# Folding the row normalisation into the attention phase that follows it

## The chip, the core and the metric

The kernel runs on one core of a Trainium2 chip. The metric is the device time of one launch in microseconds (us), here the median of several runs on one chip. The core has five engines that run their own instruction streams and meet at semaphores: TensorE (PE in the profile, with its weight loads as PEld), VectorE (DVE), ScalarE (ACT), GpSimd (POOL) and SyncE (SP), whose stream here holds only DMA issues.

## The reference

Two layers, each a cross attention added to the residual rows and a feed-forward part added to them, over x of 4 batches, 512 rows, 256 columns, and a context of 4 batches, 1024 rows, 192 columns. Each part reads normalised rows:

```python
def _layernorm(x, axis=-1, eps=1e-05):
    m = jnp.mean(x, axis=axis, keepdims=True)
    v = jnp.var(x, axis=axis, keepdims=True)
    return (x - m) / jnp.sqrt(v + eps)

# each layer, in outline
x = x + attention(_layernorm(x), context)   # 16 heads of 64; q = xn @ w_q, k, v from the context; out @ w_o + b_o
x = x + ffn(_layernorm(x))                  # layer 0: 32 experts, top 6, and 2 shared; layer 1: 8 experts, top 1, and a shared one
```

Attention is softmax(q k^T / 8) v per head. Its output bias b_o is added to every row. All data are float32.

## The kernel before

**Phases.** The program is a row of phases, each a block of its own on all engines: a normalisation (`norm_phase`, tag `n_`), attention of layer 0 (`attention_phase`, tag `L0a_`), a normalisation (`L0n_`), the experts of layer 0 (`L0e_`), a normalisation (`L1i_`), attention of layer 1 (`L1a_`), a normalisation (`L1n_`), and the experts of layer 1. A phase begins when the one before it has ended on every engine. The residual rows stay in SBUF as `xres`, 128 partitions by 16 tiles of 256; four tiles are one batch. The two normalisations ahead of the attentions, `n_` and `L1i_`, are the ones that the change takes away.

**norm_phase.** DVE takes `bn_stats` of all 16 tiles (L201), then combines them in small chained operations to a mean, a variance (L213 to L220), and, after a square root on ACT (L169), to a reciprocal with one Newton step and a shift (L222 to L228). The tiles are normalised in 8 groups of two, the even tile on DVE (L234), the odd one on ACT (L165). PE transposes a group with 4 transposes into one PSUM bank (L192). ACT copies the bank, rounded to float32r, into `xnT_hi` (L176), and DVE writes the rest, bank minus `xnT_hi`, into `xnT_lo` (L243). All products of the kernel are made of such high and low parts in three float32r matmuls. In `n_` SP loads x in two halves and the context of batch 0, which ACT (L158) and POOL (L151) split.

**attention_phase.** 32 segments, for 4 batches times 8 pairs of heads. Segment i does the attention of pair i and prepares pair i+1 and i+2. PE's order in a segment, written out by hand: transpose of the last tile of row maxima (`transpose_max`, L680), queries of i+1 (L598, six matmuls), eight `qk` steps (L696, L697) with the value projections of the next pair of segments between them, the output projection of i-1 into banks 7 and 6, then four `score` steps of i+1 (L674). A score step fills four banks, and a DVE `reduce_max` (`maximum`, L524) must have read them before the next score step may start. Between the scores lie the products with v (`pv`, L711) as `FILL` says, and after score 1 the two key projections of i+2 (ACT copies them in `high_keys` L437, DVE subtracts in `low_keys` L516). `total` (L721) ends the segment. On DVE a segment is `low_keys`, `normalise` (L529, L532), `high_queries` L503, `high_output` L538, `low_queries` L508, `low_output` L542, `add_output` L550 twice, and the four maxima with another `low_keys` ahead of the last. `add_output(i-1)` waits for the output projection.

**Start of the attention.** SP loads the packed weights of segment n into one buffer `raw`, which ACT rounds (`high_weights`, L427) and POOL subtracts (`low_weights`, L378); the load of the next one waits for that. POOL first writes rows of -1 (L413, four memsets). PE then makes keys 0, queries 0 (waiting for `low_weights(1)` and `low_keys(0, 0)`), values 0 and 1, score 0, and so on. After the four maxima of pair 0, ahead of segment 0, DVE adds the output bias to all 16 tiles of `xres` in four operations of 1024 columns (L584), from a buffer that shares its place with `inv`.

Of the kernel before, what the change touches and what calls it, by code (L numbers as in the profile page):

```python
# [7 lines left out]
ALU = mybir.AluOpType  # L8
# [4 lines left out]
P = 128  # L13
# [33 lines left out]
def build(nc, x, ctx_top, ctx_bot, layer_in, out):  # L47
# [6 lines left out]
    with stack:  # L54
# [30 lines left out]
        def norm_phase(tag, xres, source=None, keep=None, wipe=None, clear=(), prefetch=None):  # L85
# [6 lines left out]
            NCH = 2  # L92
            with scope() as s:
# [11 lines left out]
                if source is not None:  # L105
                    stage = sb(s, tag + "stage", [P, NCH, SKV])
                if wipe is not None:
                    zeros = sb(s, tag + "zeros", [P, DIM])
                sem = norm_sems | sems(
                    s, tag, ("x0 x1 id chi clo " + " ".join(f"staged{n}" for n in range(NCH)) if source is not None else "")  # L110
                    + (" zero wiped" if wipe is not None else ""))
                with nc.Block() as block:
# [6 lines left out]
                    def _(sp):  # L119
                        if source is not None:  # L120
                            for half in range(2):
                                tiles = slice(half * NG, (half + 1) * NG)
                                sp.dma_start(xres[:, tiles, :], source[:, tiles, :]).then_inc(sem[f"x{half}"], 16)
                            for n, src in enumerate((ctx_top, ctx_bot)):
                                sp.dma_start(stage[:, n, :], src[:, 0:SKV]).then_inc(sem[f"staged{n}"], 16)
# [9 lines left out]
                    def _(pool):  # L135
# [4 lines left out]
                        if source is not None:  # L140
                            nc.gpsimd.memset(ident[:, :], 0.0).then_inc(sem["id"], 1)
                            nc.gpsimd.memset(ones[:, :], 1.0).then_inc(sem["id"], 1)
                            pool.wait_ge(sem["id"], 2)
                            nc.gpsimd.affine_select(out=ident[:, :], in_=ident[:, :], compare_op=ALU.not_equal, fill=1.0, base=0,
                                                    pattern=[[-1, P]], channel_multiplier=1).then_inc(sem["id"], 1)
                            for n in range(NCH):
                                pool.wait_ge(sem["chi"], n + 1)
                                if n == 1:
                                    pool.wait_ge(sem["clo"], 1)
# [5 lines left out]
                    def _(act):  # L155
# [16 lines left out]
                        for g in range(NG):  # L172
# [5 lines left out]
                            if source is not None and g < NCH:  # L178
                                context(g)
# [1293 lines left out]
```

## Time and profile before

| what | value |
|---|---|
| median of 3 runs | 2711.11 us (2711.02 to 2711.22) |
| profiled execution, its own time | 2705.97 us |
| span of the profile (first to last instruction) | 2704.3 us |
| mean granted TensorE clock over the span | 0.966 of full speed |
| PE busy | 2521.8 us, 93% |
| DVE busy | 2145.7 us, 79% |
| POOL busy | 1531.6 us, 57% |
| ACT busy | 1212.0 us, 45% |

The busy shares are means over stages with different limits. A busy PE is not a PE at its peak, because matmuls are pipelined and their ends are modelled; starts are the better reading. The time outside the span is 1.7 us.

### The profile page before, as it was taken

How to read it: one execution, taken by the hardware profiler on the slowest of the kernel's cores; microseconds unless marked ns; L12 is line 12 of the kernel's file. 1: busy time of each engine (PE TensorE's matmuls, PEld its weight loads, DVE VectorE, ACT ScalarE, POOL GpSimd, SP SyncE). 2: the span in 40 equal slices, each digit the busy share in tenths (PEclk: the TensorE clock that was granted, in tenths of full speed). 3: DMA queues.
4: the chain of work that ended last, by engine and by line, in shares of the span. 5: the costliest groups of instructions: out<-in, count | busy, mean ns of one | idle time of the engine just before them, and what ended most of it. 6: DMA issues, size and time to landing. Idle time of an engine off the chain costs nothing. (4 is left out here: it accounts for less than half of the span.)

```text
span 2704.3 us, 37384 instructions
## 1 busy us (share of the span) xinstructions
PE 2521.8 (93%) x13062; PEld 1767.6 (65%) x13062; DVE 2145.7 (79%) x2528; ACT 1212.0 (45%) x1712; POOL 1531.6 (57%) x1132
## 2 busy tenths in 40 slices
PE   4999999999999599999999779999999999986895
PEld 3656566665656378888888656666565666645784
DVE  5788888888888577777777758888888888866795
ACT  3545444544545233333333345455454545433384
POOL 2877887878787311111111058788878778770345
PEclk8999999999999799999999879999999999997997
DMA  3221222222221100000000031222222121204112
GB/s 110 58 53 44 67 49 54 59 61 48 65 54 39 58 24 23 23 23 23 23 23 23 6 89 45 57 51 65 48 61 61 44 57 44 51 20 193 61 53 88
DMA packets 115459, 141.88 MB, mean 52 GB/s; under 512 B 63744, under 2 KB 76928, under 8 KB 114304
## 3 DMA queue, kind: packets, MB, share of 16 engines
q1 hardware_dynamic: 110480, 132.95, 18.5%
q0 software_dynamic: 1536, 4.20, 0.5%
q10 hardware_dynamic: 3312, 3.02, 0.3%
q8 instruction: 78, 1.28, 0.2%
q14 instruction: 53, 0.43, 0.1%
HBM read 79.36 MB, written 10.22 MB: 33 GB/s over the span
## 5 line engine op out<-in xcount | busy, mean ns | idle before, releaser
L397 POOL TENSOR_TENSOR L0a_psums<-L0a_psums,L0a_probs 128x512 f32<-128x512 f32 x384 | 498.1, 1334 | 3.0 <-ACT L0a_probs L454 3.0
L397 POOL TENSOR_TENSOR L1a_psums<-L1a_psums,L1a_probs 128x512 f32<-128x512 f32 x384 | 497.9, 1332 | 2.8 <-ACT L1a_probs L454 2.8
L524 DVE TENSOR_REDUCE L1a_row_max<-psum 128x2 f32<-128x2048 f32 x128 | 293.5, 2293 | 75.3 <-PE psum L674 74.3
L524 DVE TENSOR_REDUCE L0a_row_max<-psum 128x2 f32<-128x2048 f32 x128 | 293.5, 2293 | 75.2 <-PE psum L674 74.2
L890 POOL TENSOR_TENSOR L0e_w_lo<-L0e_raw,L0e_w_hi 128x768 fp32r<-128x768 f32 x34 | 63.7, 1874 | 497.3 <-ACT L0e_w_hi L904 497.3
L454 ACT ACTIVATE L0a_probs<-psum 128x1024 f32<-128x1024 f32 x256 | 251.9, 1027 | 106.3 <-PE psum L697 106.3
L454 ACT ACTIVATE L1a_probs<-psum 128x1024 f32<-128x1024 f32 x256 | 251.9, 1027 | 106.3 <-PE psum L697 106.3
L944 DVE SCALAR_TENSOR_TENSOR xres<-psum,L0e_weights_of,xres 128x256 f32<-128x256 f32 x544 | 225.5, 477 | 22.7 <-PE psum L1117 21.8
L711 PE MATMUL psum<-L1a_probs,L1a_v 128*64 128x512 f32 x1024 | 240.5, 601 | 0.0
L711 PE MATMUL psum<-L0a_probs,L0a_v 128*64 128x512 f32 x1024 | 240.4, 601 | 0.0
L1103 PE MATMUL psum<-xnT_hi,L0e_w_hi 128*128 128x512 f32 x544 | 214.1, 394 | 5.1 <-DVE L0e_hid L952 5.0
L1103 PE MATMUL psum<-xnT_lo,L0e_w_hi 128*128 128x512 f32 x544 | 213.3, 392 | 0.0
L1103 PE MATMUL psum<-xnT_hi,L0e_w_lo 128*128 128x512 f32 x544 | 211.7, 389 | 0.0
L696 PE MATMUL psum<-L0a_q_hh,L0a_k_st 128*128 128x512 f32 x512 | 204.9, 400 | 1.6 <-ACT L0a_probs L454 1.1
L696 PE MATMUL psum<-L1a_q_hh,L1a_k_st 128*128 128x512 f32 x512 | 204.8, 400 | 1.5 <-ACT L1a_probs L454 1.1
L697 PE MATMUL psum<-L0a_q_lm,L0a_k_hs 65*128 65x512 f32 x512 | 204.5, 399 | 0.0
L697 PE MATMUL psum<-L1a_q_lm,L1a_k_hs 65*128 65x512 f32 x512 | 204.5, 399 | 0.0
L915 ACT ACTIVATE L0e_act_g<-psum 128x512 f32<-128x512 f32 x136 | 81.3, 598 | 243.8 <-PE psum L1103 243.8
L550 DVE TENSOR_TENSOR xres<-psum,xres 128x512 f32<-128x512 f32 x128 | 88.5, 692 | 104.8 <-PE psum L598 103.4
L397 POOL TENSOR_TENSOR L1a_psums<-L1a_probs 128x512 f32<-128x512 f32 x64 | 81.7, 1297 | 157.3 <-ACT L1a_probs L454 157.3
L952 DVE TENSOR_TENSOR L0e_hid<-psum,L0e_act_g 128x512 f32<-128x512 f32 x136 | 93.6, 688 | 94.4 <-ACT L0e_act_g L915 94.1
L397 POOL TENSOR_TENSOR L0a_psums<-L0a_probs 128x512 f32<-128x512 f32 x64 | 81.6, 1296 | 150.5 <-ACT L0a_probs L454 150.5
(357 smaller groups left out, 6072.9 us busy)
## 6 DMA issues: line engine op xcount, KB each, us to landing
L0a_k_hs<-L0a_k_st SPq DMA_DIRECT2D x64, 256.0 KB, 3.7
L1a_k_hs<-L1a_k_st SPq DMA_DIRECT2D x64, 256.0 KB, 3.7
L0a_raw<-in_attention SPq DMA_DIRECT2D x35, 384.0 KB, 3.5
L1a_raw<-in_attention SPq DMA_DIRECT2D x35, 384.0 KB, 3.4
L0e_raw<-in_experts SPq DMA_DIRECT2D x34, 384.0 KB, 3.1
L1weights<-in_sorted SPq DMA_DIRECT2D x2, 6144.0 KB, 18.0
L0a_q_hh<-L0a_q_hh SPq DMA_DIRECT2D x64, 128.0 KB, 2.3
L1a_q_hh<-L1a_q_hh SPq DMA_DIRECT2D x64, 128.0 KB, 2.3
```

The source lines that it names most:

```text
L397: nc.gpsimd.tensor_tensor(psums[:, h, :], a, probs[:, h, kv, :], ALU.add).then_inc(sem["acc"], 1)
L454: nc.scalar.activation(probs[:, h, 2 * kp:2 * kp + 2, :], slot(h).rearrange("p (n q) -> p n q", n=2), ACT.Exp, scale=SCALE)\
L524: nc.vector.reduce_max(row_max[:, qt, 0:2 * 32].rearrange("p (h n) -> p h n", h=2)[:, :, 0], psum[:, 0:4 * BANK].rearrange("p (h k) -> p h ...
L550: nc.vector.tensor_tensor(rows, bank(PLACE[f"OUT{half}"]), rows, ALU.add).then_inc(sem["added"], 1)
L696: nc.tensor.matmul(dst, k_st[:, par, h, keys_of], q_hh[:, par, h, :], start=True, stop=False)
L697: last = nc.tensor.matmul(dst, k_hs[0:DH + 1, par, h, keys_of], q_lm[0:DH + 1, par, h, :], start=False, stop=True)
L711: last = nc.tensor.matmul(O[HEAD[h], :], v[:, pair % 2, kv, cols], probs[:, h, kv, :], start=kv == 0, stop=kv == KVT - 1)
L890: nc.gpsimd.tensor_tensor(w_lo[:, par, :], raw[:, par, :], w_hi[:, par, :], ALU.subtract)\
L915: nc.scalar.activation(act_g[:, u % 2, :], bank(u % 2), ACT.Silu).then_inc(sem["silu"], 1)
L944: last = nc.vector.scalar_tensor_tensor(acc, bank(4 + 2 * (u % 2) + n // 2)[:, (n % 2) * DIM:(n % 2 + 1) * DIM], weights_of[:, ds(j * (2 * ...
L952: nc.vector.tensor_tensor(hid[:, u % 2, :], bank(2 + u % 2), act_g[:, u % 2, :], ALU.mult)\
L1103: last = nc.tensor.matmul(bank(2 * g + u % 2), a[:, par, w], m[:, kd, rows], start=n == 0, stop=n == 3 * KD - 1)
```

## The change

The phases `n_` and `L1i_` are taken out, and `attention_phase` normalises its own rows. Batch 0 is normalised at the start of the attention beside the first weights, its transposes in banks 0 and 1. The three other batches are prepared during the segments: for batch b+1, with i mod 8 counted inside batch b, DVE takes the statistics in segment 0, the variance in segment 1 (ACT takes the root there, then runs a tiny exponential), the scales in segment 2; in segments 2 and 3 ACT normalises two tiles each, PE transposes them after the first three `pv` steps into bank 7, ACT copies, and DVE subtracts between its second and third maximum; in segment 4 DVE adds the bias to that batch. The bias of batch 0 is added in segment 0. `inv` and the bias no longer share a buffer. The weights of segments 1 and 2 are loaded into unused parts of `probs`, so that their loads wait for less. In layer 0 SP loads the tiles of batch 0 first and the rest later, and DVE takes over one of the two subtractions of the context. At the start PE runs 16 transposes whose results nobody reads. Keys 0 go to bank 7, POOL's memsets of -1 move behind `low_values(0)`, `high_queries(0)` moves ahead of `low_keys(0, 1)`, and `row_max` shrinks to 33 columns a tile, so that `transpose_max` takes 33 columns. The core of the diff:

```diff
@@ attention_phase, layout @@
+                    FIRST_K0 = 7
+                    STATS, ROOT, SCALES, GROUPS, BIAS = 0, 1, 2, (2, 3), 4
+                    def next_batch(i, step):
+                        return i // HP + 1 if i % HP == step and i // HP + 1 < BATCH else None
+                    def next_group(i):
+                        return 2 * (i // HP + 1) + GROUPS.index(i % HP) if i % HP in GROUPS and i // HP + 1 < BATCH else None
+                flat = probs[:, :, :, :].rearrange("p h n q -> p (h n q)")
+                bottom = flat[:, 4 * BANK:6 * BANK]
+                xn_first = flat[:, 6 * BANK:8 * BANK].rearrange("p (t d) -> p t d", d=DIM)
+                raw_of = {1: flat[:, 14 * BANK:14 * BANK + WCOL], 2: flat[:, 12 * BANK:12 * BANK + WCOL]}
@@ SP @@
+                        if source is not None:
+                            sp.dma_start(xres[:, 0:QT, :], source[:, 0:QT, :]).then_inc(sem["x0"], 16)
                         load_weights(0)
+                        if source is not None:
+                            sp.dma_start(ctx_stage[:, :], ctx_top[:, 0:SKV]).then_inc(sem["top"], 16)
+                            sp.dma_start(bottom, ctx_bot[:, 0:SKV]).then_inc(sem["bot"], 16)
+                        load_weights(1)
                         load_values(0)
-                        sp.dma_start(bias_sb, bias.partition_broadcast(P)).then_inc(sem["bias"], 16)
-                        load_weights(1)
+                        load_weights(2)
+                        sp.dma_start(bias_sb[:, :], bias.partition_broadcast(P)).then_inc(sem["bias"], 16)
+                        if source is not None:
+                            sp.dma_start(xres[:, QT:NT, :], source[:, QT:NT, :]).then_inc(sem["x1"], 16)
                         load_values(1)
@@ ACT, segment, between values and high_keys @@
+                            b, g = next_batch(i, ROOT), next_group(i)
+                            if b is not None:
+                                root(b)
+                                exponential_again()
+                            if g is not None:
+                                act.wait_ge(sem["tr"], g)
+                                for t in range(2):
+                                    normalise(xn[:, t, :], g, t)
+                                high_rows(g, PLACE["XT"])
@@ ACT, start @@
-                        high_weights(0)
+                        if source is not None:
+                            high_weights(0)
+                            high_context(0)
+                            root(0)
+                            high_context(1)
+                        else:
+                            root(0)
+                            high_weights(0)
+                        for g in range(2):
+                            normalise(xn_first[:, 2 * g + 1, :], g, 1)
+                        high_weights(1)
+                        for g in range(2):
+                            high_rows(g, g)
                         high_values(0)
                         high_keys(0, 0)
                         high_keys(0, 1)
-                        high_weights(1)
                         for n in range(4):
                             values(0, n)
+                        exponential_again()
                         high_keys(1, 0)
@@ DVE, segment @@
                                 low_output(i - 1)
+                            b = next_batch(i, STATS)
+                            if b is not None:
+                                if b == 1 and source is not None:
+                                    dve.wait_ge(sem["x1"], 16)
+                                statistics(b)
+                            b = next_batch(i, ROOT)
+                            if b is not None:
+                                variance(b)
+                            b = next_batch(i, SCALES)
+                            if b is not None:
+                                scales(b)
+                            b = 0 if i == 0 else next_batch(i, BIAS)
+                            if b is not None:
+                                add_bias(b)
+                            if i > 0:
                                 add_output(i - 1)
                             if i + 1 < SEGMENTS:
                                 for qt in range(QT):
                                     maximum(i + 1, qt)
+                                    if qt == 1 and next_group(i) is not None:
+                                        low_rows(next_group(i), PLACE["XT"])
@@ DVE, start @@
+                        statistics(0)
+                        variance(0)
+                        if source is not None:
+                            dve.wait_ge(sem["chi0"], 1)
+                            nc.vector.tensor_tensor(ctx_lo[:, 0, :], ctx_stage[:, :], ctx_hi[:, 0, :], ALU.subtract).then_inc(sem["clo0"], 1)
+                        scales(0)
+                        for g in range(2):
+                            nc.vector.tensor_scalar(xn_first[:, 2 * g, :], xres[:, 2 * g, :], rstd[:, 2 * g:2 * g + 1],
+                                                    shift[:, 2 * g:2 * g + 1], ALU.mult, ALU.add).then_inc(sem["xn_even"], 1)
+                        for g in range(2):
+                            low_rows(g, g)
                         low_keys(0, 0)
+                        high_queries(0)
                         low_keys(0, 1)
-                        high_queries(0)
                         low_queries(0)
...
-                        dve.wait_ge(sem["bias"], 16)
-                        for t in range(0, NT, QT):
-                            nc.vector.tensor_tensor(xres[:, t:t + QT, :], xres[:, t:t + QT, :],
-                                                    bias_sb.unsqueeze(1).broadcast_to([P, QT, DIM]), ALU.add).then_inc(sem["biased"], 1)
@@ PE, segment, after the pv steps that follow score 0 @@
+                                g = next_group(i)
+                                if qt == 0 and g is not None:
+                                    pe.wait_ge(sem["xn"], 2 * g)
+                                    pe.wait_ge(sem["added"], BEFORE + 2 * (i - 1) + 1)
+                                    transpose_rows(g, xn, PLACE["XT"])
@@ PE, start @@
+                        busy(16)
+                        for g in range(2):
+                            pe.wait_ge(sem["xn_even"], g + 1)
+                            pe.wait_ge(sem["xn"], g + 1)
+                            transpose_rows(g, xn_first[:, 2 * g:2 * g + 2, :], g)
                         keys(0, 0)
@@ phases @@
-        norm_phase("n_", xres, x_tiles)
-        attention_phase("L0a_", w["attention"], w["values"], w["out_bias"], xres, again=True)
+        attention_phase("L0a_", w["attention"], w["values"], w["out_bias"], xres, source=x_tiles, again=True)
...
-        norm_phase("L1i_", xres, clear=expert_sems.values())
-        attention_phase("L1a_", w["attention"], w["values"], w["out_bias"], xres, again=False)
+        attention_phase("L1a_", w["attention"], w["values"], w["out_bias"], xres, clear=expert_sems.values())
```

## Rows read from the trace of the kernel before

**Rows 1.** Timeline, PE in one segment: start, duration, engine, line, operation.

```profile
308.10 0.33 PE L680 MATMUL psum<-ident,L0a_row_max 128*128 128x128 f32 x1
308.20 0.47 PE L598 MATMUL psum<-xnT_hi,L0a_w_split 128*128 128x512 f32 x1
...
324.44 0.73 PE L674 MATMUL psum<-L0a_k_st,L0a_q_hh 64*128 64x512 f32 x4
```

**Rows 2.** Timeline, DVE in the same segment; in brackets idle time and its releaser.

```profile
320.44 1.41 DVE L550 TENSOR_TENSOR xres<-psum,xres 128x512 f32<-128x512 f32 x2 [1.53 <-PE psum L598]
...
325.21 2.29 DVE L524 TENSOR_REDUCE L0a_row_max<-psum 128x2 f32<-128x2048 f32 x1 [1.09 <-PE psum L674]
328.39 2.29 DVE L524 TENSOR_REDUCE L0a_row_max<-psum 128x2 f32<-128x2048 f32 x1 [0.89 <-PE psum L674]
```

**Rows 3.** Timeline, start of layer 0.

```profile
6.81 2.71 DVE L201 BATCH_NORM_STATS2 n_stats<-xres 128x6 f32<-128x256 f32 x8 [6.67 <-DMA xres<-in_x]
9.76 2.71 DVE L201 BATCH_NORM_STATS2 n_stats<-xres 128x6 f32<-128x256 f32 x8 [0.24 <-DMA xres<-in_x]
...
20.14 1.05 ACT L158 ACTIVATE ctx_hl<-n_stage 128x1024 fp32r<-128x1024 f32 x1
...
37.08 0.80 PE L598 MATMUL psum<-ctx_hi,L0a_w_split 128*128 128x512 f32 x1 [7.72 <-POOL L0a_w_split L378]
...
52.34 2.30 DVE L524 TENSOR_REDUCE L0a_row_max<-psum 128x2 f32<-128x2048 f32 x1 [1.41 <-PE psum L674]
```

**Rows 4.** Timeline, normalisation of layer 1 and the first weights.

```profile
1531.02 5.32 DVE L201 BATCH_NORM_STATS2 L1i_stats<-xres 128x6 f32<-128x256 f32 x16 [0.32 <-PEq L836]
1536.38 0.18 DVE L213 TENSOR_TENSOR L1i_mean<-L1i_stats 128x16 f32<-128x16 f32 x1
...
1538.09 0.22 ACT L169 ACTIVATE L1i_std<-L1i_var 128x16 f32<-128x16 f32 x1 [5.81 <-DVE L1i_var L220]
...
1539.74 1.09 ACT L165 ACTIVATE L1i_xn<-xres,L1i_shift,L1i_rstd 128x256 f32<-128x256 f32 x2 [1.44 <-DVE L1i_shift L228]
...
1540.48 1.94 PE L192 MATMUL psum<-ident,L1i_xn 128*128 128x128 f32 x8 [11.48 <-DVE L1i_xn L234]
...
1552.72 0.34 SPq L330 DMA_DIRECT2D L1a_raw<-in_attention  x1
...
1555.89 0.84 ACT L427 ACTIVATE L1a_w_split<-L1a_raw 128x768 fp32r<-128x768 f32 x1 [4.16 <-DMA L1a_raw<-in_attention]
```

**Rows 5.** Timeline of layer 1: first key product, first maximum.

```profile
1558.81 0.79 PE L598 MATMUL psum<-ctx_hi,L1a_w_split 128*128 128x512 f32 x1 [7.71 <-POOL L1a_w_split L378]
...
1574.48 2.29 DVE L524 TENSOR_REDUCE L1a_row_max<-psum 128x2 f32<-128x2048 f32 x1 [1.56 <-PE psum L674]
```

**Rows 6.** Timeline, the bias of layer 0, PE's wait in segment 0.

```profile
65.47 6.26 DVE L584 TENSOR_TENSOR xres<-xres,L0a_inv 128x1024 f32<-128x1024 f32 x4
...
73.30 0.48 PE L598 MATMUL psum<-L0a_wv,ctx_hi 128*128 128x256 f32 x2 [1.66 <-DVE L0a_k_st L516]
```

**Rows 7.** Stretches: busy of PE, PEld, DVE, ACT, POOL; then granted clock.

```profile
45.10:50.40 5.30, 5.26 (x18) 4.68 (x19) 2.22 (x4) 0.16 (x1) 1.21 (x1) 0.50 0.57 147
...
74.20:77.80 3.60, 3.60 (x12) 2.90 (x11) 1.77 (x3) 1.52 (x2) 1.10 (x1) 0.53 0.32 73
...
1540.00:1552.00 12.00, 8.21 (x32) 5.86 (x32) 7.37 (x16) 8.20 (x16) 0.00 (x0) 0.50 0.00 0
```

**Rows 8.** Timeline, PE in the slow stretch of 45.10 to 50.40.

```profile
47.01 0.63 PE L598 MATMUL psum<-xnT_lo,L0a_w_split 128*128 128x512 f32 x1
...
47.44 0.63 PE L598 MATMUL psum<-xnT_hi,L0a_w_split 128*128 128x512 f32 x1
```

**Rows 9.** Timeline, ACT: table load, and idle time ahead of `high_keys`.

```profile
56.89 2.42 ACT L437 ACTIVATE L0a_k_st<-psum 64x512 fp32r<-64x512 f32 x4 [1.44 <-PE psum L598]
...
67.81 1.28 ACT L454 ACT_TABLE_LOAD   x1
...
326.56 2.42 ACT L437 ACTIVATE L0a_k_st<-psum 64x512 fp32r<-64x512 f32 x4 [5.42 <-PE psum L598]
```

More of the change, by code:

```diff
@@ L139, in _ @@
                             nc.gpsimd.memset(zeros[:, :], 0.0).then_inc(sem["zero"], 1)
[L140 to L149, printed above, removed]
-                                part, hi, lo = ((slice(0, P), ctx_hi, ctx_lo), (slice(DH, P), ctx_hl, ctx_hl))[n]
-                                nc.gpsimd.tensor_tensor(lo[part, 0, :], stage[part, n, :], hi[part, 0, :], ALU.subtract)\
-                                    .then_inc(sem["clo"], 1)
                     @block.scalar
                     def _(act):
-                        def context(n):
-                            act.wait_ge(sem[f"staged{n}"], 16)
-                            nc.scalar.activation((ctx_hi, ctx_hl)[n][:, 0, :], stage[:, n, :], ACT.Copy).then_inc(sem["chi"], 1)
                         def normalise(g):
@@ L548, in add_output, with statistics @@
                                 dve.wait_ge(sem["out"], 2 * i + half + 1)
+                                if i % HP == 0 and half == 0:
+                                    dve.wait_ge(sem["biased"], i // HP + 1)
                                 dve.wait_ge(sem["added"], BEFORE + 2 * (i - 1) + half + 1)
                                 nc.vector.tensor_tensor(rows, bank(PLACE[f"OUT{half}"]), rows, ALU.add).then_inc(sem["added"], 1)
+                        def statistics(b):
+                            for t in range(QT):
+                                nc.vector.bn_stats(stats[:, t, :], xres[:, b * QT + t, :]).then_inc(sem["stat"], 1)
+                            dve.wait_ge(sem["stat"], QT * (b + 1))
@@ L739, in output, with transpose_rows, busy @@
                             last.then_inc(sem["out"], 1)
+                        def transpose_rows(g, rows, place):
+                            for t in range(2):
+                                for k in range(KD):
+                                    last = nc.tensor.transpose(group_bank(place)[:, k, t * P:(t + 1) * P], rows[:, t, k * P:(k + 1) * P],
+                                                               ident[:, :])
+                            last.then_inc(sem["tr"], 1)
+                        def busy(times):
+                            for _ in range(times):
+                                nc.tensor.transpose(bank(3)[:, 0:P], ident[:, :], ident[:, :])
                         def segment(i):
```

166 lines of the change are left out of this document (120 added, 46 removed).

## The prediction, made before the changed kernel was run

> **What bounds the kernel now.** I read the page first: no engine but PE is near full, and the granted clock is full except in a few slices, one of them the first. The change touches two normalisation phases and both attentions, so the next view is the timeline of one segment, PE beside DVE. The reader should see there who starts whom. On PE, score 1 of the next pair starts at 324.44 [rows 1]. On DVE the first maximum ends 1.09 us ahead of the start of the second at 325.21, so at 324.12, and it is DVE that idles until PE delivers score 1; the second ends at 327.50 and DVE idles another 0.89 us for score 2, which is behind the key projections on PE [rows 2]. From `transpose_max` to score 2 PE's own order sets the pace, from there DVE's does. Work put on PE between score 0 and score 2 is therefore paid in full. DVE has three gaps in a segment: 1.53 us ahead of `add_output`, 1.09 us and 0.89 us ahead of the second and third maximum. A delay of the first maximum costs nothing below 0.32 us, since PE is ready for score 1 only at 324.44.
>
> The third view is the timeline of the starts. Here nothing overlaps: in layer 0 PE makes its first key product at 37.08 and DVE its first maximum at 52.34 [rows 3]; in layer 1 the normalisation begins at 1531.02, the attention's first load is issued at 1552.72 [rows 4], keys start at 1558.81 and the first maximum at 1574.48 [rows 5]. Last come the stretches with their clock [rows 7].
>
> **What is removed at the start of layer 1.** The new chain, from 1531.0. Statistics of 4 tiles instead of 16: 5.32/16 = 0.33 each, 1.4 with the tail. Six small chained operations at 0.21 (eight of them take 1536.38 to 1538.09 [rows 4]): 1.3, so the variance is there at 1533.7. From root to scales 1.65 (1538.09 to 1539.74 [rows 4]): 1535.4. From scales to the first transpose 0.7, and eight transposes 1.94 [rows 4]: 1538.1. Beside it the weights take 3.17 from issue to ACT (1552.72 to 1555.89 [rows 4]) and at most 2.92 from there over ACT and POOL to PE at 1558.81 [rows 5]; even behind the root on ACT they are ready at 1537.1, so the transposes end last. Keys start at 1538.1 instead of 1558.81: 20.7 us earlier. The memsets of -1, which stood ahead of the first `low_weights`, are wanted only much later; the 16 idle transposes take at most 16 x 0.24 and end at 1534.9, before the rows come.
>
> **At the start of layer 0.** x comes in two halves of 1 MB; the first is used at 6.81 and the second at 9.76 [rows 3], 2.95 us per MB. So the 0.5 MB of batch 0 land at 6.81-1.5 = 5.3, the weights (384 KB) at 6.4, the context's first half (512 KB) at 7.9, its second at 9.4. DVE has the variance at 5.3+1.4+1.3 = 8.0. ACT does weights, then the first context half (1.05 [rows 3]) until 9.0, then the root until 9.2. DVE subtracts the context meanwhile, 1.4 (I take two of its 512-column operations, L550 [rows 2]): 10.4. Scales 1.3: 11.7; to the end of the transposes 0.7+1.94: 14.4. POOL's half of the context can start when ACT has done its own at 10.4; for 768 columns of weights ACT and POOL together took 2.92 [rows 5], so 1024 columns take at most 3.9, and it is no later. Keys start at 14.4 instead of 37.08: 22.7 us.
>
> **From the first keys to the first maximum.** Before: 15.3 us in layer 0 and 15.7 in layer 1 [rows 3, 5]. New: 10 key and 6 query matmuls, then `high_queries` and `low_keys(0, 1)` on DVE one behind the other (2 x 1.4, two operations of 512 columns each [rows 2]), a new wait: in the old order both keys were done by the time the queries came. Then 20 value matmuls of 256 columns and a score, 0.9. The matmuls depend on the clock. In 45.10:50.40 it was 0.50, which is 1.2 GHz, after PE had idled, and a matmul of 512 columns took 0.43 from start to start (47.01 to 47.44 [rows 8]): 16 x 0.43 = 6.9, and 20 x 0.21 = 4.3 for the values; at 2.4 GHz about half of it, 3.6 and 2.3. So 14.9 at the low level and 9.6 at the high one. I take 12.4, near the middle: PE is busy soon after the phase starts, but with transposes and with pauses. That gains 2.9 and 3.3, together 6.2 (1.2 to 11.8). The Trainium skill (TensorE: Matmul & The Clock Gate, Part 1) says that the throttled clock is the default and sustained activity releases it; by that the two starts lie nearer to the high level once keys and queries run without a pause, and the sum would be some 2 us larger. The trace agrees only in so far as 45.10:50.40 was slow after an idle PE.
>
> **Bias.** Four operations, 6.26 us, stand ahead of the first `low_keys` of segment 0, and PE idles 1.66 us for it; right behind, PE runs 3.6 us at a clock of 0.53 [rows 6, 7]. Without it 1.66 goes for sure, and up to half of 3.6 with it. I take 2.5 per layer, 5.0 (3.3 to 6.9). Statistics and bias of 1.4 and 1.6 (6.26/4) come later in segment 0, ahead of a first maximum that waited for PE for many microseconds there.
>
> **Table load.** `exponential_again` puts a table load of 1.28 and a tiny exponential of about 0.2 (as the root, 0.22 [rows 4]) into a gap of 1.44 ahead of `high_keys(1, 0)` [rows 9]: nothing lost. The Trainium skill (ScalarE: Activation LUTs, What ACT_TABLE_LOAD costs) adds a drain of about 1.38 us to each switch of set. By it `high_keys(1, 0)` comes 1.4 late in each layer and the sum loses 2.8; no row here shows a drain that holds anything. In the segments with a root, two loads, 0.4 of work and even two such drains end about when ACT's idle 5.42 us do [rows 9].
>
> **What is added in the segments.** Three batches in two layers, six times:
> - statistics 1.4, variance 1.3, scales 1.3 on DVE, each in the 1.53 us gap ahead of `add_output`: nothing. Bias 1.6: 0.1 over, under the 0.32 above.
> - Two groups: two ACT operations of 0.55 after 321.1, when its values are out (326.56-5.42 [rows 9]), done by 322.3, ahead of the transposes at about 324.4. Four transposes on PE: 0.10 from L680's start to the next matmul [rows 1], 0.12 as half of the 0.24 (1.94/8 [rows 4]) at the low clock of 1540.00:1552.00 [rows 7]; 0.5 a group. They stand between score 0 and score 1, so they are paid: 12 x 0.5 = 6.0. At the low clock's price with a wait it is 1.0 each, 12.
> - `low_rows`, 0.7 (as one operation of L550 [rows 2]), between the second and third maximum: the gap is 0.89, so it is hidden. With a score 2 that comes as late as the second maximum ends it would be 0.7 x 12 = 8, but both shift together.
>
> Inserts and `low_rows` may still overrun by up to 0.3 in 12 places, 3.6. If 0.1 us of cover is gone in any of them, the next thing late is the maximum, then the score behind it on PE.
>
> **Sum.** 20.7+22.7+6.2+5.0-6.0 = 48.6, against the profiled execution's own 2705.97: about 2657. The median of the runs stands 5.1 above that, so I forecast 2711.1-48.6 = 2662.5, say 2662. Smallest gain: 43.4+1.2+3.3-12-3.6 = 32.3, 2679; largest: 43.4+11.8+6.9-5.0 = 57.1, 2654.
>
> **Rivals.**
> (1) The starts are held by something that I count as hidden: DMA landings. All early loads share one queue; if batch 0, weights, context and the second weights land as late as all of it did before (second half of x used at 9.76, context behind it), layer 0 gains some 6 less, and if the pause before the values lets the clock fall, 5 more are lost in both layers. 2662+11 = 2673. For it: the queue was the first thing waited for [rows 3]. Against: less is in front.
> (2) The gaps of DVE don't hide the inserts, because a chain of waits moves with them. Then each batch pays 1.4+1.3+1.3+1.4+1.6 = 7.0, six times 42: 2704. Against: the releaser of every gap is PE.
> (3) Slower: the change makes PE stop in each altered segment (30 of them: five per batch, six times), because its next score or the transposes wait, and its clock falls. The price is the one of segment 0: 1.66 idle and half of 3.6 slow, 3.4 us, times 30 = 102, 2764. It decides from 48.6/30 = 1.6 us a segment. The same page of the Trainium skill tells of a PE that micro-idles between groups and swings between the two clocks. For it: the slow stretch behind the bias [rows 7]. Against: the waits that I find are well under 1.66.
> (4) The change only trades waits: what it puts ahead of the first keys holds them as long, and nothing moves; 2711.
>
> **How the numbers follow.** A difference under 0.2% (5.4 us) can't be told from none. Forecast 0.74, (1) 0.12, (2) 0.08, (3) 0.04, (4) 0.02. The range starts at 2652, a little under the bound of 2654, and reaches past (1) to 2682, leaving out (2), (3) and (4). (2) at 2704 is still faster by 0.26%, but near the edge, so 0.02 of it goes to the same. Faster 0.92, same 0.04, slower 0.04.
>
> **What would show it.** First key product at about 14.4 us and about 7 us into the attention of layer 1; first maximum some 25 us and 24 us earlier; no L584-like block ahead of segment 0; segments with transposes 0.5 us longer and all other altered ones as before; the gap ahead of `add_output` closed but the maximum behind it on time. I am wrong if altered segments grow by a microsecond or more, if the granted clock drops in them, or if keys 0 wait for a load.

## The result and the profile after

The changed kernel is slower: 2746.09 us median of 4 runs (2745.64 to 2746.37) against 2711.16 on the same chip, a ratio of 1.0126 [1.0114, 1.0138], 34.9 us more. The prediction was 2662, its range 2652 to 2682.

The page of the profile after, its busy times, and the view by core:

```profile
span 2744.7 us, 37538 instructions
...
PE 2548.0 (93%) x13094; PEld 1781.3 (65%) x13094; DVE 2218.8 (81%) x2587; ACT 1237.7 (45%) x1751; POOL 1532.8 (56%) x1129
```
```profile
core 0: 2744.7 us, clock 0.957
```

No share moved much, and the clock fell by 0.009. So I go by places. The timeline of DVE at the start of layer 0, which answers to [rows 3]:

```profile
4.83 1.41 DVE L625 BATCH_NORM_STATS2 L0a_stats<-xres 128x6 f32<-128x256 f32 x4 [3.70 <-DMA xres<-in_x]
...
27.40 2.29 DVE L593 TENSOR_REDUCE L0a_row_max<-psum 128x2 f32<-128x2048 f32 x1 [2.14 <-PE psum L822]
```

PE's first key product of both layers (answers to [rows 3, 5]), and DVE's first statistics and first maximum in layer 1 ([rows 4, 5]):

```profile
15.55 0.78 PE L741 MATMUL psum<-ctx_hi,L0a_w_split 128*128 128x512 f32 x1
...
1555.74 0.78 PE L741 MATMUL psum<-ctx_hi,L1a_w_split 128*128 128x512 f32 x1
```
```profile
1547.19 1.40 DVE L625 BATCH_NORM_STATS2 L1a_stats<-xres 128x6 f32<-128x256 f32 x4
...
1568.78 2.29 DVE L593 TENSOR_REDUCE L1a_row_max<-psum 128x2 f32<-128x2048 f32 x1 [3.62 <-PE psum L822]
```

The starts came nearly as forecast: the first maximum of layer 0 is 24.9 us earlier (52.34 to 27.40). To measure the rest I use one event that every segment has, the `reciprocal` of the row sums on DVE (128x512, 3.36 us). From one to the next is the length of a segment. The first one of layer 0 came at 98.50 before and at 70.16 after, 28.3 earlier. From the last one of layer 0 to the first of layer 1 it was 710.59 and is 684.59, 26.0 less. Together the starts gave 54.3; the prediction had 54.6 for them (48.6 plus the 6.0 that it deducted inside the segments).

The loss lies between the first and the last reciprocal of each attention: 811.53 became 855.74 in layer 0, 811.47 became 854.87 in layer 1, 87.6 us more. Lengths in us, worked out from those starts. Each step comes in three segments of each layer, six in all (of the six segments with statistics, two lie ahead of the first reciprocal and aren't measured this way):

| segment | before | after | six times |
|---|---|---|---|
| statistics | 26.4 | 26.4 | 0 |
| variance | 26.4 | 32.1 to 32.8 | +36.6 |
| scales, first group | 26.4 | 33.3 to 33.6 | +42.7 |
| second group | 26.4 | 26.9 | +3.3 |
| bias | 26.4 | 26.7 | +1.8 |

The second-last segment of each layer has 26.2 instead of 24.5, 3.4 in all. It has no part of the change in it, and several other kernels below show it at either length in either layer. So 54.3 gained and 87.6 lost are 33.3 lost. What follows the attention of layer 1 is 7.1 longer in this pair of profiles, 279.3 against 272.2. Nothing of the change lies there; the other profiles of kernels with the change have between 273.4 and 282.3, and no run here shows why. The two profiles differ by 40.4; the profiled run of before lies 5.2 under its median, so the medians differ by 34.9.

What happens in a variance segment, DVE and beside it POOL:

```profile
78.11 1.49 DVE L611 TENSOR_TENSOR L0a_o_split<-L0a_inv,L0a_o_split 128x512 fp32r<-128x512 f32 x1
79.52 1.25 DVE L636 TENSOR_TENSOR L0a_total_of<-L0a_stats 128x4 f32<-128x4 f32 x1
80.69 0.16 DVE L637 TENSOR_TENSOR L0a_var<-L0a_stats 128x4 f32<-128x4 f32 x1
80.77 1.26 DVE L638 TENSOR_TENSOR L0a_dif<-L0a_stats 128x4 f32<-128x4 f32 x1
82.06 1.20 DVE L639 SCALAR_TENSOR_TENSOR L0a_dif<-L0a_dif 128x4 f32<-128x4 f32 x1
83.29 1.19 DVE L640 TENSOR_TENSOR L0a_var<-L0a_var,L0a_dif 128x4 f32<-128x4 f32 x1
84.52 1.20 DVE L641 TENSOR_SCALAR L0a_var<-L0a_var 128x4 f32<-128x4 f32 x1
85.74 1.29 DVE L621 TENSOR_TENSOR xres<-psum,xres 128x512 f32<-128x512 f32 x2
86.95 2.28 DVE L593 TENSOR_REDUCE L0a_row_max<-psum 128x2 f32<-128x2048 f32 x1
90.06 2.29 DVE L593 TENSOR_REDUCE L0a_row_max<-psum 128x2 f32<-128x2048 f32 x1 [0.83 <-PE psum L822]
94.81 2.29 DVE L593 TENSOR_REDUCE L0a_row_max<-psum 128x2 f32<-128x2048 f32 x1 [2.45 <-PE psum L822]
```
```profile
75.07 15.51 POOL L408 TENSOR_TENSOR L0a_psums<-L0a_psums,L0a_probs 128x512 f32<-128x512 f32 x12
```

Six operations on 128x4 take 6.2 us (79.52 to 85.74), five of them about 1.2 each; the trace says busy, not waiting. They start 1.2 apart, in step with POOL's sums of the probabilities: a train of twelve that follow each other without a pause at 15.51/12 = 1.29. The view of one tile shows the same operations where POOL is idle and where it isn't (ns: min/median/max):

```profile
L638 DVE TENSOR_TENSOR L0a_dif<-L0a_stats x4: 160/1256/1261, 6.4 to 531.0; 128x4 f32<-128x4 f32 x4
L639 DVE SCALAR_TENSOR_TENSOR L0a_dif<-L0a_dif x4: 164/1195/1195, 6.6 to 532.3; 128x4 f32<-128x4 f32 x4
```

The minimum is the first batch, at the start; the other three are in segments. What it does to PE (timeline), and the stretches with the granted clock in the third-last column: 86 to 98 in the variance segment, 118 to 130 in the scales segment, and 150 to 156 in the segment of the second group, which has a step but nothing small on DVE beside POOL:

```profile
89.29 0.73 PE L822 MATMUL psum<-L0a_k_st,L0a_q_hh 64*128 64x512 f32 x4 [4.13 <-DVE L0a_row_max L593]
```
```profile
86.00:92.00 6.00, 2.71 (x10) 1.96 (x11) 5.17 (x4) 1.45 (x2) 4.58 (x4) 0.88 0.03 0
92.00:98.00 6.00, 6.00 (x25) 2.48 (x24) 3.50 (x4) 4.68 (x7) 0.19 (x1) 0.84 0.29 55
118.00:124.00 6.00, 3.07 (x11) 1.99 (x12) 4.63 (x4) 1.67 (x3) 4.70 (x4) 0.77 0.04 3
124.00:130.00 6.00, 6.00 (x20) 3.20 (x21) 3.32 (x3) 3.21 (x5) 0.45 (x1) 0.66 0.07 11
150.00:156.00 6.00, 6.00 (x32) 3.18 (x30) 4.05 (x4) 2.98 (x6) 6.00 (x6) 1.00 0.05 3
```

`add_output` and the first maximum come late, PE idles 4.13 ahead of score 1, and its clock then falls below full (0.88 and 0.84 of it in the two stretches, 1.00 from 150 to 156). The second and third maximum are 4.75 apart (90.06 to 94.81) instead of 3.18 [rows 2], 1.6 more at the lower clock. The account of this segment: 6.2 of operations, less the gap of 1.53 and the slack of 0.32, make 4.4; with 1.6 for the clock 6.0; measured 5.8.

### The profile page after: what moved, and what is told of

Its sections match the earlier page's. It is cut to its first block and busy times, and to the rows that moved or that the text cites. A ratio compares the mean times of both kernels' runs of the same rounds, so it can differ in the third digit from the quotient of the medians.

```text
span 2744.7 us, 37538 instructions
## 1 busy us (share of the span) xinstructions
PE 2548.0 (93%) x13094; PEld 1781.3 (65%) x13094; DVE 2218.8 (81%) x2587; ACT 1237.7 (45%) x1751; POOL 1532.8 (56%) x1129
## 3 DMA queue, kind: packets, MB, share of 16 engines
q8 instruction: 78, 1.28, 0.2%
## 5 line engine op out<-in xcount | busy, mean ns | idle before, releaser
L1291 PE MATMUL psum<-L0e_w_hi,L0e_hid_hi 128*128 128x256 f32 x544 | 153.3, 282 | 0.9 <-DVE L0e_hid_lo L1131 0.9
```

Of the source, the lines that this page charges most:

```text
L1291: last = nc.tensor.matmul(dst, a[:, u % 4, rows], b[:, par, w], start=m == 0, stop=m == 2)
```

## The experiments

The diffs are shortened to the lines that carry the edit; waits and some conditions are left out. Two theories. **Held:** a DVE operation of a certain kind that starts beside a POOL operation ends only when that one ends. **Semaphores:** small chained operations in a segment are slow for their waits, whatever POOL does.

**e1, POOL's sums cut to one column in the altered segments.**

```diff
+ if kv > 1 and i % HP in (ROOT, SCALES) and i // HP + 1 < BATCH:
+     nc.gpsimd.tensor_tensor(psums[:, h, 0:1], a[:, 0:1], probs[:, h, kv, 0:1], ALU.add).then_inc(sem["acc"], 1)
+ else:
      nc.gpsimd.tensor_tensor(psums[:, h, :], a, probs[:, h, kv, :], ALU.add).then_inc(sem["acc"], 1)
```

> The changed kernel, but in the segments with the variance and the scales (i mod 8 = 1 and 2, three batches) POOL's sums of the probabilities after the first two are made over 1 column instead of 512; that part of the sums is left out. Theory 'held': a small DVE operation beside a running POOL tensor operation ends only when POOL's does, so with almost no POOL work the ten slow ones (1.05 to 1.26 us) take 0.16 to 0.2 as they do at the start of layer 1, the two segments fall from 32.1 and 33.6 us to about 26.4 and 26.9, and the kernel from 2746 to 2746-6x(5.8+6.7) = 2671. Rival 'semaphores': the time is that of a wait on DVE's own semaphore while all engines are busy; then nothing changes, 2746.

Measured: 2669.12 us, ratio to the kernel before 0.9842 [0.9825, 0.9859]. This kernel leaves out most of the sums in those segments, so it is of use for its time alone. The variance segments have 26.37, scales 26.92. DVE's timeline of the same place:

```profile
78.32 0.16 DVE L642 SCALAR_TENSOR_TENSOR L0a_dif<-L0a_dif 128x4 f32<-128x4 f32 x1
78.52 0.18 DVE L643 TENSOR_TENSOR L0a_var<-L0a_var,L0a_dif 128x4 f32<-128x4 f32 x1
78.73 0.17 DVE L644 TENSOR_SCALAR L0a_var<-L0a_var 128x4 f32<-128x4 f32 x1
80.98 1.40 DVE L624 TENSOR_TENSOR xres<-psum,xres 128x512 f32<-128x512 f32 x2 [2.08 <-PE psum L744]
```

The chain and its waits are the same, each takes 0.16 to 0.18 again, and PE's clock from 82 to 94 is 1.00. Held is right, semaphores fall.

**e2, each of those sums in two halves.**

```diff
+ for c in (slice(0, SEQ // 2), slice(SEQ // 2, SEQ)):
+     last = nc.gpsimd.tensor_tensor(psums[:, h, c], a[:, c], probs[:, h, kv, c], ALU.add)
+ last.then_inc(sem["acc"], 1)
```

> The changed kernel, but in the same segments each of POOL's sums after the first two is made in two operations of 256 columns. Theory 'held, to the end of the POOL operation': the wait follows the length of one POOL operation, so the small DVE operations take about 0.65 to 0.75 us instead of 1.2, the variance takes about 4 us instead of 6.2, and the two segments come to about 29 and 30 us: 2746-6x6.5 = about 2707. A rival with a fixed price per operation beside a busy POOL, or the rival 'semaphores', leaves 1.2 us and 2746.

Measured: 2674.24, ratio 0.9861 [0.9844, 0.9878]. DVE and POOL:

```profile
79.34 0.70 DVE L643 TENSOR_TENSOR L0a_dif<-L0a_stats 128x4 f32<-128x4 f32 x1
80.08 0.66 DVE L644 SCALAR_TENSOR_TENSOR L0a_dif<-L0a_dif 128x4 f32<-128x4 f32 x1
80.77 0.67 DVE L645 TENSOR_TENSOR L0a_var<-L0a_var,L0a_dif 128x4 f32<-128x4 f32 x1
```
```profile
75.18 11.05 POOL L410 TENSOR_TENSOR L0a_psums<-L0a_psums,L0a_probs 128x256 f32<-128x256 f32 x15
```

Half a POOL operation (11.05/15 = 0.74), half the duration (0.66 to 0.70): the length of the POOL operation is the price. The segments, though, have 26.9 and 27.1, not the 29 to 30 that I expected. The halves also shorten what DVE does ahead of the block, so that it starts 8.4 us after the reciprocal (70.28 to 78.64), where DVE went idle at 9.4 before (309.50 to 318.90). The six operations take 3.5 (78.64 to 82.16), `add_output` is 0.9 late, 0.6 behind the slack of 0.32, and PE hardly stops.

**e3b, which operations are held.** e3, the first version, had forms of 128x256 as well and gave no time, because their scratch tiles didn't fit into SBUF. e3b is the kernel before, with four operations on 128x4 in the gap of segments 8 to 15 of layer 0, another kind in each; chained by semaphores but for one.

```diff
+ low_output(i - 1)
+ price(i)   # 8: tensor_tensor, 9: tensor_scalar, 10: scalar_tensor_tensor, 11: reciprocal, 12: tensor_copy,
+            # 13: tensor_tensor without chain, 14: reduce_max, 15: memset; four of each on probe tiles
  add_output(i - 1)
```

> The kernel before, with four additional DVE operations of 128x4 on a scratch tile in layer 0's gap ahead of add_output, one form per segment from segment 8 to 15: chained tensor_tensor, tensor_scalar, scalar_tensor_tensor, reciprocal, tensor_copy, then four tensor_tensor without waits between them, reduce_max, memset. Theory 'held': tensor_tensor, tensor_scalar and scalar_tensor_tensor take about 1.2 us each, reciprocal 0.17 as in the changed kernel, and the four without waits pay once (one of 1.2, three of 0.16). Rival 'semaphores': every chained form takes 1.2, reciprocal too, and the four without waits take 0.16 each.

Measured: 2724.88 in one run (before 2706.67). The view of the tile; the first line has the four chained `tensor_tensor` and the four without a chain together:

```profile
L570 DVE TENSOR_TENSOR L0a_probe<-L0a_probe x8: 150/1210/1258, 291.7 to 444.0; 128x4 f32<-128x4 f32 x8
L572 DVE TENSOR_SCALAR L0a_probe<-L0a_probe x4: 1195/1204/1259, 322.6 to 326.4; 128x4 f32<-128x4 f32 x4
L574 DVE SCALAR_TENSOR_TENSOR L0a_probe<-L0a_probe x4: 1195/1210/1249, 353.5 to 357.2; 128x4 f32<-128x4 f32 x4
L576 DVE RECIPROCAL L0a_probe<-L0a_probe x4: 163/178/179, 384.4 to 385.0; 128x4 f32<-128x4 f32 x4
L578 DVE COPY L0a_probe<-L0a_probe x4: 1194/1203/1256, 410.7 to 414.5; 128x4 f32<-128x4 f32 x4
L580 DVE TENSOR_REDUCE L0a_probe<-L0a_probe x4: 143/157/157, 468.5 to 469.1; 128x1 f32<-128x4 f32 x4
L582 DVE MEMSET L0a_probe<- x4: 62/62/62, 495.0 to 495.4; 128x4 f32 x4
```

Held: `tensor_tensor`, `scalar_tensor_tensor`, `tensor_scalar` and `tensor_copy` between SBUF tiles, 1.20 each, in segments of 30.9. Not held: reciprocal, maximum and memset, segments of 26.4. Without the chain four `tensor_tensor` take 2.58 together and the segment 26.9. I expected one of 1.2 and three of 0.16; 2.58 is the length of two POOL operations, so two of the four pass behind each. The Trainium skill (SBUF — State Buffer, Who interferes with whom) has this rule: VectorE and GpSimd share one pair of SBUF ports, a VectorE instruction with two SBUF inputs, or a copy or `tensor_scalar` in a mode with two ports, contends with a GpSimd instruction that reads SBUF, and the second to start is blocked until the first has finished. The trace agrees for each kind tried here, with 1.20 beside 1.29 of POOL; the long casts under e4 and e6 go beyond it. This rule speaks against the change, and the prediction didn't weigh it.

**e5, the bias alone.** The kernel before with the bias added per batch, as in the change.

```diff
- for t in range(0, NT, QT): nc.vector.tensor_tensor(xres[:, t:t + QT, :], ...)   # ahead of segment 0
+ b = 0 if i == 0 else i // HP + 1 if i % HP == 4 and i // HP + 1 < BATCH else None
+ if b is not None: nc.vector.tensor_tensor(rows, rows, bias_sb[:, :].unsqueeze(1).broadcast_to([P, QT, DIM]), ALU.add)
```

> The kernel before with one part of the change alone: the bias has a buffer of its own and is added per batch, batch 0 in segment 0 and the others in segment 4 of the batch before, ahead of add_output, instead of in one block ahead of segment 0. By the prediction's terms PE's wait of 1.66 us goes and up to 1.8 us of the low clock behind it, twice, and nothing is paid in the segments: 2711-5 = 2706 (2704 to 2708). By what the changed kernel showed the bias beside POOL takes 2.3 us instead of 1.6 and its segment 0.3 us more, 6x0.3: 2708. If the clock behind the wait was not the wait's doing, 2711-3.3+1.8 = 2709.5.

Measured: 2703.14, ratio 0.9987 [0.9978, 0.9996], 3.5 us less than before on the same chip. That is nearer to the second expectation (3 less, with the bias held) than to the first (5 less). From the first maximum to the first reciprocal the profile has 4.1 less in layer 0 and 3.4 less in layer 1; six segments have 0.3 more.

**e4, the small operations on POOL itself.** If POOL's operations hold them, POOL can do them: variance and scales behind its sums, about 0.2 each; only the reciprocal stays on DVE.

```diff
+ b = next_batch(i, STATS)       # POOL, end of its segment; the scales likewise in the segment of ROOT
+ if b is not None:
+     pool.wait_ge(sem["acc"], ACCS * (i + 1))
+     pool.wait_ge(sem["stat"], QT * (b + 1))
+     plink(nc.gpsimd.tensor_tensor(total_of[:, :], me, mo, ALU.add))   # and five more, then var
```

> The changed kernel, but for batches 1 to 3 the small operations of variance and scales run on POOL, behind the last sum of segments 0 and 1, where POOL idles; only the reciprocal stays on DVE, behind the second maximum of segment 1. 'Held': DVE has nothing small left beside POOL's sums; the segments of 32.1 and 33.6 us become 26.4 and 26.9, and the kernel comes to 2746-6x(5.8+6.7) = 2671, 40 us faster than before the change. If instead the place in PE's and ACT's order (root with two table loads, rows normalised on ACT) makes these segments long, they stay above 30 us and the kernel above 2710.

Measured: the profiled run 2668.60, all segments as expected, but seven of the eight runs lie between 2668.60 and 2702.76 and the eighth at 2710.84, median 2685.46; the seven give a ratio of 0.991 [0.9882, 0.9939]. The same kernel once more:

> The kernel with the small operations on POOL once more, because eight runs of it lay between 2668.6 and 2710.8 us while its profiled execution had every segment at the expected length. If the spread comes from the chip in that quarter of an hour, this one's runs all lie within 5 us of 2669; if it is the kernel's own, they spread again, and a slow execution in the profile would show which segments grow.

Measured: 2663.32 to 2689.75 in six runs, median 2677.98, ratio 0.9882 [0.9854, 0.991]: the spread is the kernel's own. This time the profile caught one long segment, 42.1 us instead of 26.4. DVE and POOL there, and PE's idle time:

```profile
1599.07 3.36 DVE L629 RECIPROCAL L1a_inv<-psum 128x512 f32<-128x512 f32 x1
...
1604.50 14.91 DVE L638 CAST L1a_o_split<-L1a_inv 128x512 fp32r<-128x512 f32 x1
```
```profile
1600.03 1.85 POOL L389 TENSOR_TENSOR L1a_w_split<-L1a_raw,L1a_w_split 128x768 fp32r<-128x768 f32 x1
1601.85 2.54 POOL L408 TENSOR_TENSOR L1a_psums<-L1a_probs 128x512 f32<-128x512 f32 x2
1604.35 14.78 POOL L408 TENSOR_TENSOR L1a_psums<-L1a_psums,L1a_probs 128x512 f32<-128x512 f32 x12
```
```profile
1621.61 2.93 PE L769 MATMUL psum<-L1a_w_split,L1a_o_split 128*128 128x256 f32 x12 [12.35 <-DVE L1a_o_split L642]
```

A cast of 1.05 us was held not by one sum but by all twelve, until POOL had no more. The sums took 1.23 each here, 1.30 where DVE gets in between. One such event costs some 15 us. A different number of them per execution would explain the scatter; only the profiled runs show it, with none in 2668.60 and one in 2682.60. Ahead of that segment's sums POOL does the subtraction of the context and the small operations, and the sums start without the usual pause of 3 us, 2.8 us after the reciprocal instead of 2.4. The same holds in every segment of that place, 18 in the three profiles of e4, e4c and e6; two of the 18 have the event.

**e6, two more edits on top of e4:** in layer 0 POOL's half of the context waits for the scale, and in layer 1 ACT normalises all four first tiles, since DVE's two tiles, beside POOL's `low_weights`, had taken 3.79 us there instead of 0.73.

```diff
+ pool.wait_ge(sem["scale"], 1)                          # layer 0, ahead of ctx_hl
+ normalise(xn_first[:, 2 * g, :], g, 0)                 # ACT, layer 1, instead of DVE's tensor_scalar
```

> The kernel with the small operations on POOL, and two holds at the starts taken away: in layer 0 POOL's half of the context waits until DVE has its scales (so the last small operation doesn't wait 2.1 us for POOL's 2.34), and in layer 1 ACT normalises all four tiles (so DVE's two don't wait for POOL's two weight subtractions, 3.79 instead of 0.73). 'Held' expects keys 0 about 2 us earlier in layer 0 and 1 to 1.5 us earlier in layer 1: 3 us below the kernel with the small operations on POOL in like runs, 2665 beside 2668. If these waits are hidden by others, the same.

Measured: 2664.32, six runs from 2662.37 to 2681.25, ratio 0.9844 [0.9831, 0.9857]; one segment of 41.4 in the profile, again one cast, of 14.94. The total came as expected, but not by the terms expected. In layer 1 the first keys come 6.8 us after the statistics' start instead of 7.4, 0.6 and not 1 to 1.5. In layer 0 they come at 16.32, against 15.36 and 16.83 in the two profiles of e4: with POOL's context half moved behind the scales, DVE's two tiles fall beside it and take 4.46.

```profile
11.03 4.46 DVE L748 TENSOR_SCALAR L0a_probs<-xres,L0a_rstd,L0a_shift 128x256 f32<-128x256 f32 x2 [0.15 <-DVE L0a_shift L685]
11.12 2.34 POOL L465 TENSOR_TENSOR ctx_hl<-L0a_probs,ctx_hl 64x1024 fp32r<-64x1024 f32 x1 [2.66 <-DVEq L686]
```

The hold was moved, not removed. Runs of e4c reach 2663.32 without these two edits, so a gain of their own isn't shown.

**e7, e6 with the steps two segments later**, away from POOL's context work.

```diff
- STATS, ROOT, SCALES, GROUPS, BIAS = 0, 1, 2, (2, 3), 4
+ STATS, ROOT, SCALES, GROUPS, BIAS = 2, 3, 4, (4, 5), 6
```

> The changed kernel with the small variance and scales operations on POOL behind its sums, POOL's context half waiting for the scale in layer 0, all four first tiles of layer 1 normalised on ACT, and, new here, the steps moved two segments later (statistics in segment 2, variance behind 3's, groups in 4 and 5, bias in 6), so that no segment has both POOL's context subtraction and POOL's links in it. Theory 'POOL late': the single segments of 41 to 42 us came where the links and the context subtraction made POOL start its sums late, so that they ran as one gapless train of about 14.8 us with a DVE operation held behind it. Then no segment is above 27.0, all runs lie within 0.2% of each other, and the median is about 2663 (2660 to 2666). Theory 'POOL's links themselves': the links alone still make the sums late now and then; a third or more of the runs lie 12 to 45 us higher and the median is about 2670 to 2685.

Measured: 2663.87, five runs from 2662.85 to 2666.18, ratio 0.9841 [0.9828, 0.9855]. No segment is above 26.94, and in all of them but the last of each layer the sums start 2.4 us after the reciprocal again. All five runs beat both kernels, the one before by 42 us. Five of the six runs of e6 lie as low (2662.37 to 2667.39), so five runs alone don't prove that the event is gone.

**e8 and e9, is a late POOL enough to shut out DVE?** Both are the kernel before with extra subtractions of weights on POOL, which write the same values again. e8 sets them in eight segments, e9 in 40 with a swept width. WCOL is 768 columns.

```diff
+ for w in widths:    # e8: 1 to 4 times WCOL; e9: WCOL two or three times and one of 300 to 706 columns
+     nc.gpsimd.tensor_tensor(w_split[:, par, 1, 0:w], raw[:, 0:w], w_split[:, par, 0, 0:w], ALU.subtract).then_inc(late, 1)
  low_weights(i + 3)
```

> The kernel before, with 1, 2, 3 and 4 extra subtractions of 768 columns (about 1.85 us each, the same result written again) on POOL ahead of its sums, in segments 8 and 10, 12 and 14, 16 and 18, 20 and 22 of layer 0. In the kernel before POOL waits 3.06 us for the first exponentials ahead of the sums. Theory 'gapless train': with 1 extra, POOL is still early or just in time and the segment stays at 26.4; from 2 extra on the sums start late, run without gaps for 10 us or more until they have caught up with ACT, and the DVE cast or subtraction of the output that meets them is held for the length of that train: segments of 30 to 42 us in some of these six. Theory 'only one POOL operation holds': DVE is never held for more than one POOL operation of 1.23 us; the six segments stay under 28 us, and the total under 2720.

Measured: 2708.77, ratio 1.001 [1.0001, 1.002]; the longest of the eight segments has 26.6 and the one behind it 27.1, though POOL's sums started up to 6.8 us after the reciprocal instead of 2.4, without a pause ahead of them. All ten runs lie between 2708.32 and 2715.74.

> The kernel before, with three or four extra subtractions on POOL ahead of its sums in 42 segments of the two layers (not in the first two of each batch, where POOL has the context to subtract); the width of one of them grows in steps of 16 or 18 columns, so that the start of the sums is swept by about 1.2 us past the cast of the output on DVE. Result the same as before. In 18 segments of three profiles this cast met a sum 0.14 to 0.19 us after the sum's start, and twice it was then held for the whole train of 12 sums (14.9 us); at 0.5 us, in all other segments, it never was. Theory 'phase': whether DVE gets in at the end of a sum depends on how shortly after a sum's start its instruction comes; then some of the segments with an offset under 0.2 us are 38 us or longer, and none at other offsets, total 2720 to 2850. Theory 'something else of those segments' (POOL's links or the context subtraction in front): no segment is longer than 28 us, total under 2725.

Measured: 2716.45 in one run. The edit reached 40 segments, not 42, and all have 26.3 to 26.5. One of them, with the cast 0.09 us behind the start of a sum, DVE and POOL:

```profile
423.51 1.49 DVE L549 CAST L0a_o_split<-L0a_inv 128x512 fp32r<-128x512 f32 x1
```
```profile
423.42 15.60 POOL L408 TENSOR_TENSOR L0a_psums<-L0a_psums,L0a_probs 128x512 f32<-128x512 f32 x12
```

The cast ends 1.58 after the sum's start here, and 1.57 in the usual case (1.05 long, 0.53 behind): it is done soon after the one sum is. Eight casts were under 0.2 us behind a sum's start, six of them behind the first of the twelve; none was held for a second one. Lateness alone didn't bring the event in the ten runs of e8. For the phase e9 says less: if the event came in one of nine such segments, as in 2 of 18 above, eight casts would miss it four times in ten (an estimate, 16/18 to the eighth power). The event was seen only with the small POOL operations and the context subtraction ahead of the sums; what in it decides stays open.

## Why the prediction was wrong

**The step that failed** is "statistics 1.4, variance 1.3, scales 1.3 on DVE, each in the 1.53 us gap ahead of `add_output`: nothing". For statistics it held (26.4). For variance and scales the duration was wrong: 0.21 a piece came from rows where POOL idles [rows 4], and the gap lies beside POOL's sums. Six operations measured 6.2 instead of 1.3, and the segments lost 5.7 to 7.2 each: 36.6 for the variance and, without the 3.3 of the first groups, 39.4 for the scales, together 76.0 us. Without them 2746.1 becomes 2670, and e1 measured 2669.12. The prediction named the signs of its being wrong, and two of the three came: altered segments longer by over a microsecond, and a lower clock in them.

The trace of before had the sign. Timeline of DVE, first beside POOL's sums, then at the end of layer 0's attention, where POOL is idle:

```profile
317.42 1.48 DVE L542 TENSOR_TENSOR L0a_o_split<-L0a_inv,L0a_o_split 128x512 fp32r<-128x512 f32 x1
...
914.61 0.69 DVE L542 TENSOR_TENSOR L0a_o_split<-L0a_inv,L0a_o_split 128x512 fp32r<-128x512 f32 x1
```

One instruction of one shape with two durations, 1.48 and 0.69, wants an explanation before its neighbourhood is taken for free.

**Rivals.** The loss is that of rival (2) in its place and rival (3) in its effect: the inserts weren't hidden, PE stopped for 4.1 us, and its clock fell, in 12 segments and not in 30, at 6.3 instead of 3.4 each. Both put the cause in waits; it was an operation that took longer, so both had a chance that was too small. Rival (1) didn't come: x was used at 4.83 and the keys waited for no load. Rival (4) neither.

**Start of layer 0.** Keys at 15.55 instead of 14.4. The same mechanism is in it: two small operations beside POOL's first weights and its context half took 1.75 and 2.30 (L640, L650) instead of 0.16. What one hold alone costs isn't shown, since e6 and e7 take the second away and have keys at 16.32 and 16.26, with DVE's tiles held in its place. The working also left out ACT's table load of 1.28 ahead of the root; the root ran at 9.46 where the forecast had it end at 9.2, and that was hidden. First maximum 24.9 earlier; forecast 25.6. From keys to maximum it took 11.9, and 13.0 in layer 1, where 12.4 was forecast.

**Start of layer 1.** Forecast: keys 7.1 after the statistics' start; measured 8.6 (1547.19 to 1555.74), with DVE's two tiles at 3.79 beside POOL's weights. In e1, which has the same start, the tiles took 1.99, the keys came after 7.3, and the first maximum against the last reciprocal of layer 0 is 24.1 earlier, as forecast (24.0). In the changed kernel's own profile it is 21.6 earlier (664.45 to 642.88). How long DVE is held there differs from profile to profile.

**Bias and what follows the first maximum.** From it to the first reciprocal the time fell by 3.4 and 4.4, forecast 2.5 each. e5, with the bias alone, gives 4.1 and 3.4 there. So this term was sized too small, and it made up for what the starts missed: that their sum came out right is in part luck.

**Groups.** 0.55 a segment where 0.5 was forecast: right. Bias in segments: forecast 0, measured 0.3, a single operation held (2.31 instead of 1.6). The table loads and `low_rows` cost nothing that a segment shows: e1's variance segments, which have two loads each, are 26.37 long. Nor does the drain show: in layer 0 the load at 8.17 ends at 9.45 and the root starts at 9.46.

**Net.** With the small operations out of POOL's way the change gives most of what was forecast: 42 us in e1 and in e7, against 48.6. In e7 the missing 6.5 are small terms, by e7's profile: the starts gave 53.6 instead of 54.6, and the segments took 10.0 instead of 6.0 (groups 6.6, bias 1.8, one second-last segment 1.7), and the rest of the span took 1.5.

## What to carry to other kernels

A duration belongs to what runs beside it: before putting VectorE work into a gap, look what GpSimd does in that gap, and price each copy, `tensor_scalar` or operation with two SBUF inputs at one GpSimd operation if they are chained. Small work can go to GpSimd itself, behind its long operations (e4, e7; then look at the spread of the runs and not at one time alone), or GpSimd's operations can be cut in two (e2). Moving work to a place beside another GpSimd operation only moves the hold, as in layer 0 of e6. An operation that shows two durations at one shape in the trace of before is the sign to look for.

## What was not expected of the hardware

A VectorE operation can be held for a whole train of GpSimd operations, not only for one: 14.91 and 14.94 us beside twelve sums of 1.23, twice in three profiles of kernels with the small GpSimd operations in the context segments; in e9 it did not come in 40 trains behind added POOL work. Seven runs of such a kernel (e4) spread by 34 us (2668.60 to 2702.76), the five of e7 by 3.3.
